# A three-stage kernel's weight preparation merged into its attention block, with the weights' peaks taken in the stage before and one restacking transfer moved ahead of another

## The chip, the cores and the metric

The kernel runs on one core of one Trainium2 chip. The metric is the device time of one execution in microseconds (us); lower is better. A core has a matrix engine (TensorE, here PE, with its weight loads as PEld), a vector engine (VectorE, DVE), a scalar engine (ScalarE, ACT), GpSimd (POOL), and SyncE (SP), which here only issues DMAs. Each runs its own instruction list in order, and they wait for each other through semaphores.

## The reference

```
h = ssm_kernel(log_dt, Lambda, x, L=1024)        # (32, 128, 1024), real part of a sum over 64 modes
h = concatenate([h, txt], axis=1)                # (32, 205, 1024)
h = h + attention(layernorm(h), wq, wk, wv, wo)  # 32 query heads, 8 key heads, head size 32, causal
h = h + ffn(layernorm(h), W_base, ...)           # a 1024x1024 map plus a low-rank one turned by an inverse FFT
```

wq is 1024x1024, wk and wv are 1024x256. `ssm_kernel` makes, for each of 32 images and 128 rows, 1,024 samples of a sum of decaying waves. The text has 77 rows an image, so an image has 205 rows in all.

## The kernel before

The program is a row of blocks. Within a block the engines run side by side; at its end all of them wait for each other.

**State-space block** (`ssm`). After some tables (the first 64 us) a loop over 16 chunks of 8 rows runs. In each chunk ACT copies a factor `ab` (L229), DVE multiplies two tables into `es` (L360) and adds the two halves of `u` (L364) that POOL made (L191, L192), PE multiplies them (L380), ACT copies the result out of PSUM to `ob` (L237) and SP stores it to `hcat` with four DMAs (L171). `es`, `u`, `ab` and `ob` have two buffers each, so ACT may write `ob` for chunk 2 only when the stores of chunk 0 have landed. Ahead of its stores SP issues the load of wq into `stage` (L166). Behind the loop DVE takes the largest absolute value of each partition of wq (L367).

**Weight block** (`prep_qkv`). SP loads wk and wv into `st_k` (L415, L416). A scale, a power of two, is made of each set's largest value over all partitions: POOL's PARTITION_ALL_REDUCE (L423), then five tiny DVE instructions. ACT writes the high fp16 part of the scaled weights in eight pieces a set (L430), and DVE the low part, what fp16 leaves over (L448).

**Attention block** (`attention`). A software pipeline over steps b from -4 to 32. In step b the engines load and normalise image b+4 or b+5, transpose image b+3 by DMA, project image b+2 to q, k and v (units "q", "k", "v" of 24 matmuls each), find the row maxima of the scores of image b+1 (units "m"), and do scores, exponentials and weighted sums for image b. A step has eight slots g; slots 0 to 3 carry an additional v or k unit. The normalisation goes round four engines: DVE statistics (L820 to L1072), POOL square-root rounds (L1079 to L687), ACT high part (L735, L737), DVE low part (L830), SP transposes (L648, L649), whose result PE takes in its first projection of step -2 (L982). `xfh` is a single buffer, and ACT casts a unit out of PSUM (L779) only behind what stands ahead of it in its list, in steps -3 and -2 the high part of the next image. PE has two PSUM banks for units, so the third unit waits until DVE has read the first (L861).

The projected rows lie four heads to a column of partitions, and SP restacks them (L596) for the score matmuls, since those want high, high and low parts of one head in one stack: 12 DMAs for each half of q (`qst`), 12 for each half of k (`kst`), 2 for the maxima of each half (L642, L643). All stand in SP's one list, 52 of them and four transposes a step. PE's row-maximum matmuls of the next step (L964) wait for the first halves of q and k, its score matmuls (L920) for the first maxima:

```
if has["qkv"]:
    wait(sp, pj_lo, base + at(rows, "q", 3) + 1)
    wait(sp, st_filled, 24 * b + 12)
    restack(Q_PARTS, qst[par], HALVES[0], q_in[0])
if has["max"]:
    wait(sp, pj_lo, base + at(rows, "m", 0) + 1)
    shift_rows(0, nxt)
if has["qkv"]:
    wait(sp, pj_lo, base + at(rows, "k", 0) + 1)
    restack(K_PARTS, kst[par], slice(0, 1), k_in[0])
```

`pj_lo` counts the units that DVE has split, `st_filled` the scores that PE has made. In step -1 SP also issues 15 loads for the blocks behind (L620). POOL fills constants at the start of the block (L658 to L681), and PE and ACT wait for them.

**Last blocks**: weight preparation for the output, then the output loop over 52 tiles of 128 rows.

## Time and profile before

| | us |
|---|---|
| median of 3 runs | 3023.08 |
| lowest and highest | 3008.07, 3027.96 |
| the profiled execution | 3040.87 |
| its span | 3039.1 |

The profile has the span, each engine's busy time, the time that each waited and for what, and the instructions in order of time. PE is the busiest engine. PEclk is the clock that was granted to PE, as a share of 2.4 GHz. By stage the span falls into the state-space block (0 to 184), the weight block (184 to 215), the attention block (215 to about 1,850) and the output blocks. The profiled execution took 17.8 us more than the median.

### The profile page before, as it was taken

The page shows a single profiled execution, that of the slowest core. Times are in us where ns is not written, and L with a number is a line of the kernel's source. Part 1 is how long each engine was busy: PE and PEld are TensorE (multiplying, and loading weights), DVE is VectorE, ACT ScalarE, POOL GpSimd, SP SyncE. Part 2 cuts the span into 40 slices and gives each one's busy share as a digit, 9 for nine tenths or more (in the row PEclk, how much of TensorE's full clock was granted, in tenths as well). Part 3 has the DMA queues.
Part 4 walks back from the last instruction along what each step waited for, and adds up shares of the span by engine and source line. Part 5 has one row for each costly group of instructions (what it writes and reads, how often), then busy time and mean ns, then how long its engine had stood idle before and what let it go on. Part 6 is the DMA issues. An engine that isn't in the chain of part 4 may idle for free. (4 is left out here: it accounts for less than half of the span.)

```text
span 3039.1 us, 71131 instructions
## 1 busy us (share of the span) xinstructions
PE 2733.4 (90%) x27520; PEld 1970.8 (65%) x27520; DVE 1939.9 (64%) x5548; ACT 1209.0 (40%) x2522; POOL 1145.9 (38%) x1816
## 2 busy tenths in 40 slices
PE   1934699999999999999999987699999999999999
PEld 1824689898898888888889873244444444444444
DVE  8863488888888878787787664444444444444443
ACT  4322265666766666666575664210110110110110
POOL 2731165665656656566565563011011011011010
PEclk9966799999999999999999976699999999999999
DMA  7642534343443443434334323254545545544543
GB/s 239 161 117 58 127 92 97 75 105 82 89 99 80 99 95 75 99 79 98 79 91 84 64 53 128 56 138 132 132 117 133 133 117 132 132 118 132 132 116 87
DMA packets 564063, 324.61 MB, mean 107 GB/s; under 512 B 500872, under 2 KB 519432, under 8 KB 563248
## 3 DMA queue, kind: packets, MB, share of 16 engines
q1 hardware_dynamic: 541216, 256.22, 36.4%
q10 hardware_dynamic: 22512, 63.84, 6.8%
q8 instruction: 220, 3.60, 0.5%
q14 instruction: 115, 0.94, 0.1%
HBM read 116.36 MB, written 80.61 MB: 65 GB/s over the span
## 5 line engine op out<-in xcount | busy, mean ns | idle before, releaser
L982 PE MATMUL psJ<-xth,qh 128*128 128x205 f16 x2048 | 524.3, 256 | 83.6 <-DMA xtl<-xfl 82.7
L707 POOL TENSOR_TENSOR pl<-p,ph 128x410 f16<-128x410 f32 (+1 forms) x512 | 506.9, 1010 | 95.6 <-ACT ph L771 95.6
L984 PE MATMUL psJ<-xth,ql 128*128 128x205 f16 x2048 | 522.8, 255 | 0.0
L983 PE MATMUL psJ<-xtl,qh 128*128 128x205 f16 x2048 | 522.7, 255 | 0.0
L702 POOL TENSOR_SCALAR_AFFINE_SELECT p<-p 128x256 f32<-128x256 f32 (+1 forms) x768 | 330.6, 436 | 496.2 <-ACT p L764 474.7
L1322 POOL TENSOR_TENSOR hb<-h,bias_sb 128x1024 f32<-128x1024 f32 x52 | 122.1, 2348 | 965.7 <-DVE h L1358 965.7
L764 ACT ACTIVATE p<-psT,escale 128x410 f32<-128x410 f32 (+1 forms) x768 | 400.9, 566 | 183.2 <-PE psT L923 118.7
L1336 ACT CAST xh<-xn 128x1024 f16<-128x1024 f32 x52 | 54.3, 1044 | 967.9 <-DVE xn L1367 967.9
L1397 PE MATMUL ps5O<-woh,ath 128*128 128x512 f16 x832 | 316.6, 381 | 28.2 <-DMA atl<-al 28.2
L771 ACT CAST ph<-p 128x410 f16<-128x410 f32 (+1 forms) x768 | 334.6, 500 | 13.0 <-POOL p L702 12.9
L1358 DVE SCALAR_TENSOR_TENSOR h<-ps5O,osc,h_in 128x512 f32<-128x512 f32 x104 | 78.0, 750 | 403.2 <-PE ps5O L1399 403.2
L853 DVE TENSOR_REDUCE mx<-psS 77x2 f32<-77x410 f32 x512 | 295.6, 577 | 54.3 <-PE psS L971 48.4
L847 DVE CUSTOM_DVE_ANT_0 seen<-psS,mask 128x128 bf16<-128x128 f32 x1024 | 235.7, 286 | 132.1 <-PE psS L964 132.0
L1398 PE MATMUL ps5O<-wol,ath 128*128 128x512 f16 x832 | 316.6, 381 | 0.0
L1397 PE MATMUL ps5F<-wfh,xth 128*128 128x512 f16 x832 | 315.4, 379 | 1.2 <-DMA xtl<-xl 1.2
L1399 PE MATMUL ps5O<-woh,atl 128*128 128x512 f16 x832 | 316.4, 380 | 0.0
L1399 PE MATMUL ps5F<-wfh,xtl 128*128 128x512 f16 x832 | 315.4, 379 | 0.0
L1398 PE MATMUL ps5F<-wfl,xth 128*128 128x512 f16 x832 | 315.4, 379 | 0.0
L950 PE MATMUL psO<-vh,ph 128*128 128x33 f16 (+1 forms) x3072 | 262.5, 179 | 4.6 <-issue 4.0
L982 PEld LDWEIGHTS psJ<-xth,qh 128*128 128x128 f16 x2048 | 202.1, 99 | 96.0 <-issue 83.0
L950 PE MATMUL psO<-vl,ph 128*128 128x33 f16 (+1 forms) x3072 | 261.3, 178 | 0.0
L950 PE MATMUL psO<-vh,pl 128*128 128x33 f16 (+1 forms) x3072 | 261.3, 178 | 0.0
(237 smaller groups left out, 6238.1 us busy)
## 6 DMA issues: line engine op xcount, KB each, us to landing
a_in<-acat SPq DMA_DIRECT2D x52, 512.0 KB, 3.8
h_in<-hcat SPq DMA_DIRECT2D x52, 512.0 KB, 4.7
qst<-qsh SPq DMA_DIRECT2D x512, 51.2 KB, 2.1
out<-y SPq DMA_DIRECT2D x51, 512.0 KB, 3.1
hcat<-ob SPq DMA_DIRECT2D x64, 256.0 KB, 4.0
xin<-hcat ACTq DMA_DIRECT2D x32, 512.0 KB
acat<-ao ACTq DMA_DIRECT2D x64, 256.0 KB
qst<-qsl SPq DMA_DIRECT2D x256, 51.2 KB, 2.1
```

Source lines behind the costliest of these rows:

```text
L702: pool.affine_select(out=v, in_=v, compare_op=ALU.is_ge, fill=0.0, base=0, pattern=[[0, v.shape[1]], [1, w]], channel_multiplier=-1).then_ ...
L707: pool.tensor_tensor(view(pl, g % 2, k), view(p32, g % 2, k), view(ph, g % 2, k), ALU.subtract).then_inc(lo_pool, 1)
L764: act.activation(view(p32, g % 2, k), ps_view(psT[(g + k) % 2], k), ACT.Exp, scale=(escale[:, 0:1] if k < 2 else escale[0:TXT, 0:1])).then ...
L771: act.copy(view(ph, g % 2, k), view(p32, g % 2, k)).then_inc(hi_done, 1)
L853: dve.tensor_reduce(dst, v, AX.X, ALU.max).then_inc(s_read, 1)
L950: m = pe.matmul(o[:, t, r, :], p, v[0:T[j], j, g, :], start=n == 0, stop=n == len(list_) - 1)
L982: pe.matmul(ps[:, 0:S], wh[:, k, c], xth[:, par, k, 0:S], start=k == 0, stop=False)
L983: pe.matmul(ps[:, 0:S], wh[:, k, c], xtl[:, par, k, 0:S], start=False, stop=False)
L984: m = pe.matmul(ps[:, 0:S], wl[:, k, c], xth[:, par, k, 0:S], start=False, stop=k == KC - 1)
L1397: pe.matmul(ps[h][:], th[:, k, :], wh[:, k, c], start=k == 0, stop=False)
L1398: pe.matmul(ps[h][:], th[:, k, :], wl[:, k, c], start=False, stop=False)
L1399: m = pe.matmul(ps[h][:], tl[:, k, :], wh[:, k, c], start=False, stop=k == KC - 1)
```

## The change

- SP issues the loads of wk and wv with that of wq, ahead of the stores of the state-space loop. `st_k` lies in a new buffer, `arena`, that attention's `p32` and `ao` and the output weights' `fm` use later. Five temporaries of the state-space block move into the unused half of `stage`.
- DVE takes the weights' peaks in twelve pieces of 128x1024, one at the end of each of the last twelve chunks. SP writes the two peaks of each partition to memory and reads all of them back into every partition ahead of the last chunk's stores.
- The weight block is gone. In the attention block DVE makes both scales at once from the peaks read back. ACT writes wq's high part behind the first two loads of rows, and that of wk and wv at the start of step -3; DVE writes the low parts behind the statistics of the first image and in slot 0 of step -3. PE waits for them ahead of its first two units.
- POOL no longer clears `xin`. The clearing of `ph` and `pl` moves to step -4 and that of a part of `p32` to step -3; `mask` is half as wide.
- In every step SP restacks the first half of the keys ahead of the first half of the queries, where before it came last. The wait for `st_filled` moves with it.

```
-def ssm(nc, x, txt, log_dt, lam, hcat, ahead, peak):
+def ssm(nc, x, txt, log_dt, lam, hcat, acat, ahead, st_k, peaks, all_peaks, peaks_in):
...
             sp.wait_ge(tab_ok, 4)
-            sp.dma_start(ahead[0], ahead[1]).then_inc(ahead[2], 16)
+            for dst, src, arrived in ahead:
+                sp.dma_start(dst, src).then_inc(arrived, 16)
             for ch in range(NCH):
+                if ch == NCH - 1:
+
+                    sp.wait_ge(peaks_ok, 1)
+                    sp.dma_start(acat[0, 0:2 * P].rearrange("(p t) -> p t", t=2), peaks[:]).then_inc(peaks_out, 16)
+                    sp.wait_ge(peaks_out, 16)
+                    sp.dma_start(all_peaks, acat[0:1, 0:2 * P].broadcast_to([P, 2 * P])).then_inc(peaks_in, 16)
 
                 sp.wait_ge(k_read, (ch + 1) * HC // 2)
...
+            def weight_peak(n):
+
+                if n == 0:
+                    dve.wait_ge(ahead[0][2], 16)
+                if n == 8:
+                    dve.wait_ge(ahead[1][2], 32)
+                src = ahead[0][0][:, n, :] if n < 8 else st_k[:, 2 * (n - 8):2 * (n - 8) + 2, :].rearrange("p k n -> p (k n)")
+                dve.tensor_reduce(pieces[:, n:n + 1], src, AX.X, ALU.max,
+                                  apply_absolute_value=True).then_inc(piece_ok, 1)
+
...
-            dve.wait_ge(ahead[2], 16)
-            dve.tensor_reduce(peak[:], ahead[0].rearrange("p k n -> p (k n)"), AX.X, ALU.max,
-                              apply_absolute_value=True)
+                if ch >= NCH - 12:
+                    weight_peak(ch - (NCH - 12))
+            dve.wait_ge(piece_ok, 12)
+            dve.tensor_reduce(peaks[:, 0:1], pieces[:, 0:8], AX.X, ALU.max)
+            dve.tensor_reduce(peaks[:, 1:2], pieces[:, 8:12], AX.X, ALU.max).then_inc(peaks_ok, 1)
...
+def attention(nc, ahead, hcat, acat, st, qkv, arena, all_peaks, peaks_in, ksc):
...
+                    sp.wait_ge(w_lo, 2 * KC)
...
                 if has["qkv"]:
 
+                    wait(sp, pj_lo, base + at(rows, "k", 0) + 1)
+                    wait(sp, st_filled, 24 * b + 12)
+                    restack(K_PARTS, kst[par], slice(0, 1), k_in[0])
                     wait(sp, pj_lo, base + at(rows, "q", 3) + 1)
-                    wait(sp, st_filled, 24 * b + 12)
                     restack(Q_PARTS, qst[par], HALVES[0], q_in[0])
                 if has["max"]:
 
                     wait(sp, pj_lo, base + at(rows, "m", 0) + 1)
                     shift_rows(0, nxt)
-                if has["qkv"]:
-
-                    wait(sp, pj_lo, base + at(rows, "k", 0) + 1)
-                    restack(K_PARTS, kst[par], slice(0, 1), k_in[0])
...
             pool.memset(mv[:], 1.0)
             pool.memset(xfh[:, 1, :], 0.0)
-            pool.memset(xfl[:, 1, :], 0.0)
-            pool.memset(xin[:, :, 1, :], 0.0).then_inc(cleared, 1)
+            pool.memset(xfl[:, 1, :], 0.0).then_inc(cleared, 1)
...
-            chain(pool.memset(ph[:], 0.0))
-            chain(pool.memset(pl[:], 0.0))
-            pool.memset(p32[:, :, 2, :], 0.0).then_inc(const_ok, 1)
+                m = pool.memset(vh[i][:, :, :, HD:HD + 1], 1.0)
+                if i < 2:
+                    chain(m)
+            m.then_inc(const_ok, 1)
...
+                    if b == -4:
+                        pool.memset(ph[:], 0.0)
+                        pool.memset(pl[:], 0.0)
+                    if b == -3:
+                        pool.wait_ge(w_lo, 2 * KC)
+                        pool.memset(p32[:, :, 2, :], 0.0).then_inc(late_ok, 1)
                     return
+                if b == 0:
+                    pool.wait_ge(late_ok, 1)
...
 
-            act.wait_ge(cleared, 1)
+            def weights_high(n):
+                if n == 0:
+                    act.wait_ge(scale_ok, 1)
+                for k in range(KC):
+                    act.activation(hi[n][:, k], st[n][:, k], ACT.Copy, scale=scs[n][:, 0:1]).then_inc(w_hi, 1)
+
             load(0, 0)
             load(1, 1)
-            act.wait_ge(const_ok, 1)
+            weights_high(0)
+            act.wait_ge(cleared, 1)
 
             def step(b, par, has):
                 base, k0 = before(b, par), odd(b, par)
                 rows = units(has)
                 n = 0
+                if b == -3:
+                    weights_high(1)
+                if b == -2:
+                    act.wait_ge(const_ok, 1)
+                if b == 0:
+                    act.wait_ge(late_ok, 1)
...
+            link = Chain(dve, w_c)
+            dve.wait_ge(peaks_in, 16)
+            link(dve.tensor_reduce(apeak[:], all_peaks.rearrange("p (q t) -> p t q", t=2), AX.X, ALU.max))
+            for n in range(2):
+                weight_scales(dve, link, apeak[:, n:n + 1], scs[n], tops[n])
+            link(dve.scalar_tensor_tensor(escale[:], scs[0][:, 1:2], float(HD) ** -0.5, ksc[:, 1:2], ALU.mult, ALU.mult))
+            dve.sem_inc(scale_ok, 1)
             dve.wait_ge(cleared, 1)
+
+            def weights_low(n):
+                for k in range(KC):
+                    dve.wait_ge(w_hi, n * KC + k + 1)
+                    dve.scalar_tensor_tensor(lo[n][:, k], st[n][:, k], scs[n][:, 0:1], hi[n][:, k],
+                                             ALU.mult, ALU.subtract).then_inc(w_lo, 1)
...
+                        if b == -4 and g == 3:
+                            weights_low(0)
                         for piece in {6: (0,), 7: (1, 2)}.get(g, ()):
                             low_part(b + 4, piece)
+                        if b == -3 and g == 0:
+                            weights_low(1)
...
+                                if b == -2 and n + which < 2:
+                                    pe.wait_ge(w_lo, KC * (n + which + 1))
```

The function `prep_qkv` is removed whole.

SP's list, in one step of the attention block before. `kst<-ksh` with `kst<-ksl` is a half of the keys, `qst<-qsh` with `qst<-qsl` a half of the queries, `mh` and `ml` are the maxima.

```order
L596 DMA qst<-qsh 32x4x205 [waits st_filled,pj_lo]
L596 DMA qst<-qsh 32x4x205 x7
L596 DMA qst<-qsl 32x4x205 x4
L642 DMA qst<-mh 1x16x205 [waits pj_lo]
L643 DMA qst<-ml 1x16x205
L596 DMA kst<-ksh 32x205 [waits pj_lo]
L596 DMA kst<-ksh 32x205 x3
L596 DMA kst<-ksl 32x205 x4
L596 DMA kst<-ksh 32x205 x4
```

And now:

```order
L571 DMA kst<-ksh 32x205 [waits st_filled,pj_lo]
L571 DMA kst<-ksh 32x205 x3
L571 DMA kst<-ksl 32x205 x4
L571 DMA kst<-ksh 32x205 x4
L571 DMA qst<-qsh 32x4x205 [waits pj_lo]
L571 DMA qst<-qsh 32x4x205 x7
L571 DMA qst<-qsl 32x4x205 x4
L616 DMA qst<-mh 1x16x205 [waits pj_lo]
L617 DMA qst<-ml 1x16x205
```

The 26 DMAs are the same; the keys now stand first and the maxima last.

```order
L678 MEMSET vh 128x16 [waits pool_c3] x3
L679 MEMSET ph 128x2460 [waits pool_c3]
L680 MEMSET pl 128x2460 [waits pool_c3]
L681 MEMSET p 128x2x410 [waits pool_c3]
L1079 ISA
L1079 TENSOR_TENSOR rs<-rs 128x2 [waits dve_ln]
```

And now the start of POOL's attention block, where the library change stands, and the end of its constants:

```order
L632 MEMSET mv 128x4
L633 MEMSET xfh 128x1024
L634 MEMSET xfl 128x1024
L635 MEMSET ident 128x128
L636 ISA [waits pool_c3]
L636 AFFINE_SELECT ident<-ident 128x128
```

```order
L648 MEMSET vl 128x528 [waits pool_c3]
L651 MEMSET vh 128x16 [waits pool_c3] x3
L1091 TENSOR_TENSOR rs<-rs 128x2 [waits dve_ln]
L1092 TENSOR_TENSOR rs<-rs 128x2 [waits pool_ln]
L1093 TENSOR_SCALAR rs<-rs 128x2 [waits pool_ln]
```

The change of library has moved from between the constants and the square root to near their start. The one for PARTITION_ALL_REDUCE in the weight block is gone with it.

DVE's list behind the scales now:

```order
L786 SCALAR_TENSOR_TENSOR escale<-qsc,ksc 128x1 [waits w_c]
L826 BN_STATS stats<-xin 128x6 [waits w_c,x_in0,cleared]
L826 BN_STATS stats<-xin 128x6 [waits dve_ln]
L827 BN_AGGR mv<-stats 128x2 [waits dve_ln]
L826 BN_STATS stats<-xin 77x6 [waits dve_ln] x2
L827 BN_AGGR mv<-stats 77x2 [waits dve_ln]
L1082 TENSOR_SCALAR rs<-mv 128x2 [waits dve_ln]
L1083 TENSOR_SCALAR rs<-rs 128x2 [waits dve_ln]
L1084 TENSOR_SCALAR rs<-rs 128x2 [waits dve_ln]
L793 SCALAR_TENSOR_TENSOR ql<-stage,qsc,qh 128x1024 [waits w_hi,dve_ln]
L793 SCALAR_TENSOR_TENSOR ql<-stage,qsc,qh 128x1024 [waits w_hi] x7
```

The low parts of the weights (`ql`) now stand behind the first image's statistics; before they stood ahead of the block.

## Rows read from the trace of the kernel before

**Rows 1.** Busy time by stage: start and end, length, then each engine, PEclk, DMA share.

```profile
177.00:260.00 83.00, 0.33 (x3) 0.24 (x3) 33.49 (x51) 20.86 (x28) 23.06 (x51) 0.53 0.30 79
...
400.00:1750.00 1350.00, 1286.88 (x19436) 1194.86 (x19437) 1081.10 (x3705) 876.70 (x1985) 814.27 (x1490) 0.99 0.40 87
```

**Rows 2.** Timeline of the weight block: start, duration, engine, line, instruction, count, [idle before, releaser].

```profile
184.56 0.40 SPq L415 DMA_DIRECT2D st_k<-in_L_attn_wk  x1
...
192.73 0.38 POOL L423 PARTITION_ALL_REDUCE apeak<-peak_q  x1 [24.34 <-issue]
...
209.94 5.38 DVE L448 SCALAR_TENSOR_TENSOR kl<-st_k,ksc,kh 128x512 f16<-128x512 f32 x8
```

**Rows 3.** Timeline of POOL from the attention block's start to the first square root's start.

```profile
215.58 0.10 POOL L658 MEMSET mv<- 128x4 f32 x1 [16.51 <-POOLq L403]
...
217.40 1.81 POOL L661 MEMSET xin<- 128x2048 f32 x1
...
219.50 0.29 POOL L663 TENSOR_SCALAR_AFFINE_SELECT ident<-ident 128x128 f32<-128x128 f32 x1 [0.16 <-POOL ident L662]
...
228.30 0.62 POOL L678 MEMSET vh<- 128x16 f16 x3
...
240.93 0.18 POOL L1079 TENSOR_TENSOR rs<-rs 128x2 f32<-128x2 f32 x1 [6.76 <-issue]
```

**Rows 4.** Timeline of all engines: the first two images up to PE's third unit.

```profile
249.44 0.72 ACT L737 ACTIVATE xfh<-xin,rs 77x512 f16<-77x512 f32 x1
...
254.65 0.17 DVE L1072 TENSOR_SCALAR rs<-rs 128x2 int32<-128x2 int32 x1
...
258.21 0.21 POOL L687 TENSOR_SCALAR nmean<-mv 128x2 f32<-128x2 f32 x1
...
259.77 0.33 PE L982 MATMUL psJ<-xth,qh 128*128 128x205 f16 x1 [82.67 <-DMA xtl<-xfl]
...
263.31 0.72 ACT L737 ACTIVATE xfh<-xin,rs 77x512 f16<-77x512 f32 x1
...
266.26 0.25 PE L982 MATMUL psJ<-xth,qh 128*128 128x205 f16 x1
```

**Rows 5.** PE's waits from 400 to 1,750 us: total, times, longest.

```profile
PE psS L964 <- issue: 31.8, 26, 2.5
```

**Rows 6.** Timeline of one step, its third slot to the next step's start.

```profile
1085.42 1.28 SPq L649 DMA_TRANSPOSE xtl<-xfl  x1
...
1088.21 0.36 DVE L861 TENSOR_TENSOR ksl<-psJ,ksh 128x205 f16<-128x205 f32 x1
...
1092.14 0.36 DVE L861 TENSOR_TENSOR qsl<-psJ,qsh 128x205 f16<-128x205 f32 x1
1092.52 1.95 SPq L596 DMA_DIRECT2D qst<-qsh  x3
...
1113.40 0.58 PE L964 MATMUL psS<-kst,qst 96*128 96x128 f16 x4 [1.75 <-issue]
```

**Rows 7.** Timeline: two rows of the state-space loop, a peak, an instruction beside a memset.

```profile
82.17 0.59 ACT L237 COPY ob<-ps 128x512 f32<-128x512 f32 x1 [0.86 <-PE ps L380]
...
88.25 2.29 DVE L360 TENSOR_TENSOR es<-tab,ab 128x2048 f32<-128x2048 f32 x1 [1.29 <-ACT ab L229]
...
194.20 4.42 DVE L438 TENSOR_REDUCE peak_k<-st_k 128x1 f32<-128x4096 f32 x1
...
227.71 0.56 DVE L1071 TENSOR_SCALAR rs<-rs 128x2 int32<-128x2 int32 x1
```

**Rows 8.** DMA issues, 75 to 80 us and 184 to 195 us: count, size each, us to landing.

```profile
hcat<-ob SPq DMA_DIRECT2D x2, 256.0 KB, 5.2
...
st_k<-in_L_attn_wv SPq DMA_DIRECT2D x1, 1024.0 KB, 8.5
```

**Rows 9.** Durations of two lines: ns min/median/max, first and last start.

```profile
L351 DVE TENSOR_TENSOR tab<-tab,stage x4: 2291/4613/4618, 42.3 to 53.6; 128x2048 f32<-128x2048 f32 x4
...
L192 POOL TENSOR_TENSOR u<-wi,gg x16: 2527/2529/4574, 46.9 to 165.9; 128x1024 f32<-128x1024 f32 x16
```

More of the change, by code:

```diff
@@ L134, in ssm @@
         stored = [sem("stored0"), sem("stored1")]
+        pieces = sb("pieces", [P, 12])
+        piece_ok, peaks_ok, peaks_out = sem("piece_ok"), sem("peaks_ok"), sem("peaks_out")
         def by_mode(w, ch):
@@ L452, in attention @@
-def attention(nc, ahead, hcat, acat, qh, ql, kh, kl, escale):
+def attention(nc, ahead, hcat, acat, st, qkv, arena, all_peaks, peaks_in, ksc):
     T = (P, TXT)
@@ L1430, in build @@
             kh, kl = sb3("kh", [P, KC, 2 * KW]), sb3("kl", [P, KC, 2 * KW])
-            qsc, escale = sb3("qsc", [P, 4], F32), sb3("escale", [P, 1], F32)
-            prep_qkv(nc, stage, peak, wk, wv, qh, ql, kh, kl, qsc, ksc, escale)
             ahead = [(stage[:], by_chunk(wo), staged), (enc[0:R0, :], enc0, in_small), (enc[R0:R, :], enc1, in_small)]
@@ L1437, in build @@
                     ahead.append((mk[n][:, :, e, :], by_chunk(m[e]), in_small))
-            attention(nc, ahead, hcat, acat, qh, ql, kh, kl, escale)
+            attention(nc, ahead, hcat, acat, (stage, st_k), (qh, ql, kh, kl), arena, all_peaks, peaks_in, ksc)
         osc, fsc = sb("osc", [P, 4], F32), sb("fsc", [P, 4], F32)
```

97 lines of the change are left out of this document (31 added, 66 removed).

## The prediction

> **What bounds the kernel now.** I read the busy time by stage first. In the long part of the attention block, 400 to 1,750 us, PE is busy 1,287 of 1,350 us, so it has 63 us to give. Between the state-space loop and the first projection, 177 to 260 us, it does nothing [rows 1]. So a change can win at most the 83 us of that gap and 63 us in the loop, and this change touches both.
>
> Next the timeline of the gap, which is one chain. The weight block starts at 184.6, its first scale waits for POOL until 192.7, and DVE ends at 215.3 (209.94 + 5.38) [rows 2]. Then the attention block starts. POOL fills constants until 228.9, clears three buffers until about 234.2 and stands for 6.76 us ahead of its first small multiply, for which the profile names no releaser. A square root takes 3.6 us (for the second image 254.82 to 258.42), so the first is ready at 244.5 [rows 3, 4]. From there it is 15.3 us over ACT, DVE and the transposes to PE's first matmul at 259.77 [rows 3, 4]. None of DVE's statistics is on that path.
>
> Last, PE's waits in the loop. One of them has half of PE's idle time: the first row-maximum matmuls of a step, 31.8 us in 26 waits, the longest 2.5 [rows 5]. The profile gives no releaser, but the code has one: they wait for the first half of the keys, which SP issues last. In the step shown SP starts the chain (queries, maxima, keys) at 1092.52, right behind the split of unit q3 (1092.14 + 0.36), and PE starts at 1113.40 after 1.75 us of idle time [rows 6].
>
> **The change, part by part.** Times are in the profiled execution's own scale.
>
> *State-space loop.* A peak over 4,096 elements took 4.42 us [rows 7], so one over 1,024 takes 1.1 to 1.25 us. DVE is idle 1.29 us in each chunk [rows 7] at just the place where the peak now stands. It fits, and I cost it at 0; if it takes 1.4 us instead, twelve chunks lose about 1 us. The 8.7 us reduction over all of wq that goes ran beside the last chunks and the last stores and was worth nothing.
> The two loads are not free. They took 8.5 us to land on an idle queue, of which about 6 are transfer [rows 8], and the stores of chunk 0 now queue behind them. Those landed 5.2 us after the issue [rows 8], at about 81 us (the last issue was near 76), and ACT took the buffer again at 82.17 without waiting for them [rows 7]. Landing at 87, ACT comes back 5 us late. PE has four PSUM banks of cover, some 5 us, and loses a few tenths; ACT's factor for chunk 4 comes 1.6 us late, against about 0.4 us of slack on DVE. I take 1.3 us lost, once (bounds 0 and 3). The peaks' way through memory is some 0.5 us in front of the last stores. The attention block so starts at 184.6 + 1.8 = 186.4.
>
> *POOL's start.* POOL is the late one there, since the scales need no DMA and no all-reduce in this block and are ready some 2.5 us in. Up to `ident` it took 3.9 us with the memset of `xin` (1.81), which goes: 2.1, so 188.5. There the library change now stands. It is what I read the 6.76 us as; the other change in the trace, ahead of the all-reduce, took at most 8.2 (184.6 to 192.73, beside the loads of wk and wv) [rows 2, 3]. I take 7.2, as row loads run beside it: 195.7. The constants took 9.4 us (219.50 to 228.92) [rows 3], less 0.6 for the halved mask: 204.5.
> But now DVE writes wq's low parts beside them, eight instructions of 1.2 us, from about 196 to 206. Before, no low part ran beside a constant. The nearest rows speak for a price: the table multiply with two operands in SBUF takes 2.29 us alone and 4.61 beside POOL's multiply, and that goes from 2.53 to 4.57 [rows 9]; and a DVE instruction on two columns took 0.56 us beside POOL's memsets, where its like took 0.17 [rows 4, 7]. So they seem to take turns. Each of the eight low parts then holds POOL up by about 1 us. Bounds 0 and 9.7; I take 8, by these rows. The constants end at 212.5, and the square root, 3.6 us as before, at 216.1.
> The Trainium skill, in "GPSIMD Engine Reference", section "Specifications", says that GpSimd shares its SBUF interfaces with VectorE and that they contend when a DVE instruction has two SBUF inputs. The low part has two. The rows above agree for POOL's multiplies; whether a memset, which reads nothing, is held up as well, no row shows with such an instruction. By the page the whole 9.7 would be lost, without it nothing.
>
> *First images.* In the trace before, image 1's square root came 1.4 us ahead of PE's start (258.42 and 259.77). Now, counted from image 0's square root: ACT's high parts end at +5.7 (250.16 - 244.49), DVE's low parts at +7.3 behind POOL's moved memsets, wk's and wv's low parts take 5.4 more (as DVE's last row of the weight block), statistics 3.9, square root 3.6: +20.2. ACT's four high parts take 5.6 us (up to 264.03), then come unit q0's cast, DVE's last low part and split: +27. Only then may PE start its third unit. Its first could start at +16, its second ends at +22.5, so PE waits some 4.5 us in between. The third unit started at 266.26 [rows 2 to 4], now at 216.1 + 27 = 243.1: 23.1 us gained. Restarting from such a pause, PE gets the lower of its two clocks, 1.2 GHz: in the gap the granted clock was 0.53 [rows 1]; a start cost about 1.5 us. Left: 21.6.
>
> *Keys first, in the filling.* The keys can go about 2 us earlier in step -2, since k0 is split one unit ahead of q3. In step 0 the maxima now come last and PE's first scores wait for them: about 1 us lost, and another 1 by the exponential table's load. Sum 0.
>
> *Keys first, in the loop.* k0 is split at 1088.57 and q3 at 1092.50 [rows 6], and SP has been waiting since its last transpose, 1086.7 (1085.42 + 1.28) [rows 6]. So the chain of 26 DMAs starts 3.9 us earlier, and q3 is ready long before its turn. It ends with the maxima, whose landing may take 0.6 us longer than that of keys: last landing 3.3 us earlier. Even the longest wait, 2.5 us, with the 0.35 us that the scores stand ahead of it, is covered. PE's 31.8 us [rows 5] should go. Some of it comes back, since ACT and DVE used the pause to catch up; some clock dips go with it, the mean granted clock being 0.99 [rows 1]. I take 29 us, bounds 8 (others take over) and 39 (all of it and the dips).
>
> **The sum.** 21.6 + 0 + 29 = 50.6 us. 3040.87 - 50.6 = 2990.3 for the profiled execution; that one stood 17.8 above the median, so 3023.08 - 50.6 = 2972.5 for the median. About 1%, 30 us, is what a measurement of this kernel can tell from no change.
>
> **Rivals.**
> 1. *Others take over in the loop.* PE's other 31 us of idle time show that ACT and DVE are near behind. If they fill most of the pause, the loop gives 8 and not 29: 2993.5. Against it: slots 0 to 3, where the pause is, are PE's longest, and ACT and DVE have room there.
> 2. *No taking turns.* Memsets don't hold DVE up and POOL's constants take what they took: 8 us more gained, 2964.5. For it: the fill of `vh` beside DVE's statistics kept its length. Against it: rows 7 and 9.
> 3. *The merged start is slower than reckoned*: a longer library change, 3 us lost in the loop of chunks, a second cold start. Some 14 us less, 2986.5.
> 4. *Slower: the maxima become the gate.* `mh` and `ml` are now SP's last issues, and they gate not only the row maxima but the step's first scores, and with them exponentials and everything behind. If SP's chain does not start earlier, because SP is still busy with transposes when k0 is split, each step gets 0.35 + 0.6 us for the later last landing and about 1 us for exponentials that no longer run in the pause: 31 steps by 1.95 = 60 us lost. 3023.1 - 21.6 + 60 = 3061.5. It decides where the chain starts less than about 1 us earlier. Against it: SP stood idle 5.8 us ahead of the chain in the step shown (1086.7 to 1092.52) [rows 6].
>
> **Chances.** The forecast 0.55, rival 1 0.17, rival 2 0.15, rival 3 0.09, rival 4 0.04. The time is that of the forecast, 2972.5. Its bounds: all terms at their best end give 8 + 1.3 + 10 = 19 us more, 2953, and some 8 for the scatter of the runs, 2946; at their worst 1.7 + 1.7 + 1 + 21 = 25 less, 2998, and a part of the scatter, 3003. That range takes in rivals 1 to 3. Faster by over 1% (below 2992.9): nearly all of the forecast, rivals 2 and 3 and half of rival 1, 0.84; within 1% 0.12; slower 0.04.
>
> **What would show each step.** In the trace of the changed kernel: ACT's first copy of chunk 2 some 5 us late and PE with a gap of about a microsecond near 95 us; no gap in the last twelve chunks; POOL's idle time of about 7 us behind `ident`; POOL's constants at 1.5 to 2 times their length beside `ql`; PE's first unit near 232 and its third near 243 with 4 to 5 us of idle time ahead of it; SP starting the keys right behind the split of k0; no wait left at the row maxima's first matmul, and none above a few tenths at the scores' (L920 before). I would be wrong if steps kept their 47 us, or if a wait for `ml` stood at each step's start.

## The result, and the profile after

The median of four runs is 2978.19 us (2973.98 to 2981.47), against 3015.57 for four runs of the kernel before beside them (3002.17 to 3027.96). The ratio is 0.9861, with a 95% interval of 0.9826 to 0.9896: faster by over 1%. The predicted 2972.5 is 5.7 us off. A second series, with 14 runs of the kernel before, gave 2968.8 for the changed kernel and 0.9813 (0.978 to 0.9847). Each kernel shows two times about 20 us apart (last section): all four runs of the changed kernel in the first series stand at its longer one, half of the four before; at equal level the gain is 47 us in the first series and 50 to 54 in the second.

The total was nearly right, but two of its terms were off by about 10 us each, in opposite directions. That shows only stage by stage.

The busy time by stage of the kernel after, with the columns of [rows 1]:

```profile
177.00:260.00 83.00, 31.26 (x294) 29.24 (x292) 40.67 (x78) 33.16 (x53) 29.69 (x61) 0.69 0.38 83
400.00:1700.00 1300.00, 1245.44 (x19005) 1161.79 (x19002) 1054.29 (x3622) 859.02 (x1938) 791.33 (x1463) 1.00 0.42 89
```

PE now works 31 us of the gap. In the loop it is idle 55 us of 1,300, or 4.2%; before it was 63 of 1,350, or 4.7%. That is a smaller step than a wait of 31.8 us that goes should make. The gap first, on POOL (to set beside [rows 3]):

```profile
187.78 0.10 POOL L632 MEMSET mv<- 128x4 f32 x1 [18.27 <-POOLq L77]
...
190.03 0.29 POOL L636 TENSOR_SCALAR_AFFINE_SELECT ident<-ident 128x128 f32<-128x128 f32 x1 [0.24 <-POOL ident L635]
...
198.38 0.61 POOL L651 MEMSET vh<- 128x16 f16 x3
198.90 1.04 POOL L1091 TENSOR_TENSOR rs<-rs 128x2 f32<-128x2 f32 x1
200.02 1.12 POOL L1092 TENSOR_TENSOR rs<-rs 128x2 f32<-128x2 f32 x1
...
208.40 0.19 POOL L1091 TENSOR_TENSOR rs<-rs 128x2 f32<-128x2 f32 x1
...
209.51 0.25 POOL L660 TENSOR_SCALAR nmean<-mv 128x2 f32<-128x2 f32 x1
...
211.78 2.14 POOL L670 MEMSET pl<- 128x2460 f16 x1
```

Look for two things. There is no idle time of 7 us anywhere, behind `ident` or elsewhere. And the same small multiply takes 1.04 to 1.12 us at 199 to 208 and 0.19 at 208.40. DVE and PE in the same stretch (to set beside [rows 4]):

```profile
198.61 9.66 DVE L793 SCALAR_TENSOR_TENSOR ql<-stage,qsc,qh 128x1024 f16<-128x1024 f32 x8
211.35 0.75 DVE L836 SCALAR_TENSOR_TENSOR xfl<-xin,rs,xfh 128x512 f16<-128x512 f32 x1 [3.09 <-ACT xfh L718]
212.72 0.75 DVE L836 SCALAR_TENSOR_TENSOR xfl<-xin,rs,xfh 128x512 f16<-128x512 f32 x1 [0.61 <-ACT xfh L718]
```

```profile
226.16 0.33 PE L992 MATMUL psJ<-xth,qh 128*128 128x205 f16 x1 [47.94 <-DMA xtl<-xfl]
...
235.71 0.26 PE L992 MATMUL psJ<-xth,qh 128*128 128x205 f16 x1 [3.04 <-DVE qsl L867]
```

The slow multiplies stand beside `ql`, whose instructions read two buffers; the memset of `pl` (211.78, 2.14 us) stands beside `xfl` (212.72), and neither is longer than its like elsewhere. PE's third unit starts at 235.71, 30.6 us earlier than before.

PE's waits in the loop, 400 to 1,700 us (total, times, longest), for [rows 5], and in the filling, 240 to 400 us:

```profile
PE psS L978 <- DVE mx L853: 38.0, 54, 1.1
PE psT L933 <- ACT arena L757: 13.9, 38, 1.8
```

```profile
PE psS L978 <- DVE mx L859: 13.9, 1, 13.9
PE psT L930 <- DMA qst<-ml: 11.6, 1, 11.6
PE psS L974 <- DMA qst<-qsl: 5.7, 1, 5.7
```

The keys' wait is gone whole. But the wait for DVE's row maxima, which in the kernel before was this one row over 400 to 1,750 us, has grown from 15.0 to 38.0:

```profile
PE psS L968 <- DVE mx L847: 15.0, 40, 1.1
```

SP's list in one step (for [rows 6]) shows why the keys' wait went: the keys start at 1099.79 and the first queries 8.4 us behind them, and the maxima come last.

```profile
1099.79 2.48 SPq L571 DMA_DIRECT2D kst<-ksh  x4
...
1108.15 5.92 SPq L571 DMA_DIRECT2D qst<-qsh  x8
1114.11 2.75 SPq L571 DMA_DIRECT2D qst<-qsl  x4
1116.91 0.60 SPq L616 DMA_DIRECT2D qst<-mh  x1
```

Two marks split the whole into start, loop and rest: PE's first and last weighted-sum matmul. Of the kernel before and of the kernel after, from their timelines of PE:

```profile
371.91 0.18 PE L950 MATMUL psO<-vh,ph 128*128 128x33 f16 x1
...
1850.04 0.19 PE L950 MATMUL psO<-vh,pl 77*128 77x33 f16 x1
```

```profile
339.26 0.18 PE L960 MATMUL psO<-vh,ph 128*128 128x33 f16 x1
...
1792.58 0.19 PE L960 MATMUL psO<-vh,pl 77*128 77x33 f16 x1
```

The start gave 32.6 us and not 21.6. The loop is 1,453 us long, and 1,478 in the profiled run of the kernel before. How much of these 25 the change made is not to be had from two profiles; e1 to e4 say it.

The busy time inside the loop shows what the rows of waits do not. Here are its first 28 images and its last four, before and after (columns as in [rows 1]):

```profile
371.91:1702.10 1330.19, 1267.80 (x19154) 1176.98 (x19153) 1073.67 (x3669) 867.63 (x1961) 806.33 (x1484) 0.99 0.41 89
1702.10:1850.04 147.94, 128.67 (x1979) 109.51 (x1978) 87.20 (x341) 91.75 (x210) 94.28 (x152) 0.77 0.23 55
```

```profile
339.26:1651.30 1312.04, 1255.81 (x19155) 1170.98 (x19154) 1073.14 (x3669) 870.46 (x1961) 800.76 (x1484) 1.00 0.42 90
1651.30:1792.58 141.28, 122.60 (x1979) 105.21 (x1978) 86.73 (x341) 91.73 (x210) 92.69 (x152) 0.83 0.24 57
```

PE does the same work, but is busy 18 us less for it (1,396.5 and 1,378.4 us), at a higher granted clock, while its idle time falls by 7 us only (81.7 and 74.9). The kernel before falls to half the clock for a few microseconds in some steps. The step of [rows 6] is one of them, where PE starts at 1113.40 behind an idle time of 1.75 us:

```profile
1113.00:1117.00 4.00, 3.60 (x25) 3.30 (x26) 1.85 (x11) 0.30 (x2) 0.92 (x3) 0.57 0.09 22
```

### The profile page after: what moved, and what is told of

It is laid out like the page before. It is cut to its first block and busy times, and to the rows that moved or that the text cites. A ratio compares the mean times of both kernels' runs of the same rounds, so it can differ in the third digit from the quotient of the medians.

```text
span 2979.7 us, 71132 instructions
## 1 busy us (share of the span) xinstructions
PE 2714.5 (91%) x27520; PEld 1960.1 (66%) x27520; DVE 1940.0 (65%) x5561; ACT 1211.3 (41%) x2522; POOL 1142.8 (38%) x1813
## 5 line engine op out<-in xcount | busy, mean ns | idle before, releaser
L992 PE MATMUL psJ<-xth,qh 128*128 128x205 f16 x2048 | 520.1, 254 | 51.9 <-DMA xtl<-xfl 47.9
L688 POOL TENSOR_TENSOR pl<-arena,ph 128x410 f16<-128x410 f32 (+1 forms) x512 | 499.9, 996 | 95.5 <-ACT ph L764 95.5
L683 POOL TENSOR_SCALAR_AFFINE_SELECT arena<-arena 128x256 f32<-128x256 f32 (+1 forms) x768 | 330.4, 436 | 476.8 <-ACT arena L757 455.2
L757 ACT ACTIVATE arena<-psT,escale 128x410 f32<-128x410 f32 (+1 forms) x768 | 401.7, 567 | 123.1 <-PE psT L933 60.8
L764 ACT CAST ph<-arena 128x410 f16<-128x410 f32 (+1 forms) x768 | 334.5, 500 | 13.5 <-POOL arena L683 13.4
L960 PEld LDWEIGHTS psO<-vh,ph 128*128 128x128 f16 (+1 forms) x3072 | 245.8, 97 | 6.7 <-issue 6.6
```

The costliest lines, as they stand in the source:

```text
L683: pool.affine_select(out=v, in_=v, compare_op=ALU.is_ge, fill=0.0, base=0, pattern=[[0, v.shape[1]], [1, w]], channel_multiplier=-1).then_ ...
L688: pool.tensor_tensor(view(pl, g % 2, k), view(p32, g % 2, k), view(ph, g % 2, k), ALU.subtract).then_inc(lo_pool, 1)
L757: act.activation(view(p32, g % 2, k), ps_view(psT[(g + k) % 2], k), ACT.Exp, scale=(escale[:, 0:1] if k < 2 else escale[0:TXT, 0:1])).then ...
L764: act.copy(view(ph, g % 2, k), view(p32, g % 2, k)).then_inc(hi_done, 1)
L960: m = pe.matmul(o[:, t, r, :], p, v[0:T[j], j, g, :], start=n == 0, stop=n == len(list_) - 1)
L992: pe.matmul(ps[:, 0:S], wh[:, k, c], xth[:, par, k, 0:S], start=k == 0, stop=False)
```

## The experiments

Twelve kernels ran. Line numbers shift by two to four between them.

### One part of the change at a time (e1 to e4)

e1 is the kernel before with the changed order of SP's list, e2 the changed kernel with the old order. e3 and e4 are the kernel after and before once more, to see how far two profiles of one kernel lie apart. The edit of e1, in `step` on SP:

```
                 if has["qkv"]:
 
+                    wait(sp, pj_lo, base + at(rows, "k", 0) + 1)
+                    wait(sp, st_filled, 24 * b + 12)
+                    restack(K_PARTS, kst[par], slice(0, 1), k_in[0])
                     wait(sp, pj_lo, base + at(rows, "q", 3) + 1)
-                    wait(sp, st_filled, 24 * b + 12)
                     restack(Q_PARTS, qst[par], HALVES[0], q_in[0])
...
-                if has["qkv"]:
-
-                    wait(sp, pj_lo, base + at(rows, "k", 0) + 1)
-                    restack(K_PARTS, kst[par], slice(0, 1), k_in[0])
```

> The kernel before with SP's order alone changed (keys, queries, maxima). Theory (the loop's wait for the keys goes, little takes its place): about 20 us less than the kernel before in the median, since the profile showed 25 us between the first and the last weighted sum and the kernel before was profiled in one of its longer executions; the wait at the row maxima's first matmul gone, the state-space and weight blocks unchanged, the first 370 us within 2 us. Rival (the maxima become the gate): 0 to 60 us more, with a wait for ml at each step's start. Second rival (other waits take the place, only ACT's and DVE's): within 8 us of before, with DVE's maxima as PE's wait grown by the 30 us that the keys' wait lost.

> The changed kernel with SP's order put back (queries, maxima, keys). Theory: the merge alone is worth what PE's third unit came earlier, 30 us (266.26 to 235.71), so 28 to 32 us less than before, and the wait at the row maxima's first matmul is back, 10 to 32 us in the loop. Rival (part of the merge's gain is lost again in the filling because SP's loads for the later blocks stand there anyway): 20 us or less. The two parts, this run and the one with the keys alone, should add up to the whole within 5 us if they are independent.

> The changed kernel again, on the same chip as the two halves. Theory: 40 to 50 us less than the kernel before, its executions within 5 us of each other, since the wait whose length varied is gone; 2974 to 2982 us.

> The kernel before, profiled once more. Its executions lie between 3002 and 3041 us. Theory (the spread is the length of the wait for the keys): an execution near 3010 us has 30 us less than the one profiled, and its wait at the row maxima's first matmul is below 15 us in total instead of 31.8. Rival (the spread comes from somewhere else, such as the clock or the output loop): the wait is near 30 us whatever the time.

Measured, in us, the kernel before at 3030.68 beside them:

| | median | ratio, 95% interval | first weighted sum | loop | PE busy, idle in it |
|---|---|---|---|---|---|
| before (profile of the first series) | | | 371.9 | 1478.1 | 1396.5, 81.7 |
| e4, before again | 3023.8 (one run) | | 369.1 | 1465.9 | 1388.7, 77.2 |
| e1, keys first alone | 3007.75 | 0.994, 0.992 to 0.9959 | 369.6 | 1455.1 | 1376.7, 78.5 |
| e2, merge alone | 2998.33 | 0.9901, 0.9866 to 0.9935 | 338.4 | 1472.0 | 1393.1, 78.9 |
| after (profile of the first series) | | | 339.3 | 1453.3 | 1378.4, 74.9 |
| e3, after again | 2968.8 | 0.9813, 0.978 to 0.9847 | 338.9 | 1451.1 | 1378.3, 72.7 |

By these marks the parts add. The three profiles without the merge start their weighted sums at 370.2 on average, the three with it at 338.8: 31.4 us. The three loops without keys first are 1472.0 long, the three with it 1453.2: 18.8 us. Neither touches the other's number. (The medians alone, 22.9 and 32.4 against 61.9, miss the 5 us that I had allowed, since half of e3's runs stand at the shorter of its two times; against those at the longer one the whole is 53.5.) The waits of e2 in the loop are those of the kernel before:

```profile
PE psS L976 <- issue: 32.6, 26, 2.2
PE psS L980 <- DVE mx L855: 13.4, 37, 1.1
```

So the wait for the maxima grows only when the keys' wait goes (39.3 us in e1). The last column says what the 18.8 us are: on average PE's idle time falls by 3.9 us and its busy time, for the same work, by 14.9. Cut into windows of 50 us from 400 to 1,700 us, the granted clock is below 1.00 in seven windows of the kernel before, in three of e4 and in four of e2, and in none of e1, after or e3. The order of SP's list alone makes this difference, with the merge and without it. So the pauses for the keys cost PE clock as well as time, and most of what their removal gave came from there. The last four images, where the clock is low for longer in all six, give some 6 of the 14.9 us; why they do was not tried.
Two profiles of one kernel differ by 12 us in the loop (before and e4), though their waits for keys differ by under 3 (30.4 and 27.7 us between 400 and 1,700); 7.8 of the 12 are busy time, again with more windows at a low clock. No single pair of profiles can size a term of 20 us. The theory of e4, that the spread is the length of the wait for the keys, is so not borne out (17 us shorter as a whole, 2.7 us less of that wait), and e3's forecast of runs within 5 us of each other failed: they span 22.

### The library of POOL (e5)

```
+            chain(pool.memset(spare_in[:], 1.0))
+            chain(pool.partition_all_reduce(spare_out[:], spare_in[:], P, RMAX))
             pool.memset(mv[:], 1.0)
```

> The changed kernel with one all-reduce over a throwaway 128x1 tile at the head of POOL's attention block, everything else as it is. Theory A (POOL pays for its library only on the way into and out of the all-reduce's, and both payments went when the all-reduce went): about 8 us more before the first identity mask, made of the switch in and the reduce of about 0.1 to 0.2 us, and 6 to 7 us of idle in front of the first tensor_tensor of the square root; the square root of image 0 is ready 13 to 15 us later than 209.8, so near 224, and PE's first product and third unit about 10 to 15 us later. Rival B (a library change is free in this kernel wherever it stands now, and the 8.1 and 6.8 us of before were something else, such as waiting for the peaks): the reduce takes under 1 us, no idle over 1 us ahead of the square root, milestones within 2 us of the changed kernel's.

POOL's timeline:

```profile
185.17 0.10 POOL L633 MEMSET spare_in<- 128x1 f32 x1 [17.48 <-POOLq L77]
192.58 0.38 POOL L634 PARTITION_ALL_REDUCE spare_out<-spare_in  x1 [7.31 <-issue]
...
195.20 0.29 POOL L639 TENSOR_SCALAR_AFFINE_SELECT ident<-ident 128x128 f32<-128x128 f32 x1 [0.16 <-POOL ident L638]
...
211.71 0.18 POOL L1094 TENSOR_TENSOR rs<-rs 128x2 f32<-128x2 f32 x1 [7.53 <-issue]
```

Theory A holds: one all-reduce on one column costs 7.31 us ahead of it and 7.53 us ahead of the first multiply behind it, though memsets, the mask and a cast stand between. The first multiply pays for the way back, not `ident`. Its sizes for what follows were too large: the square root is ready at 215.0 and not near 224, since the block started 2.6 us earlier and the multiplies, now behind `ql`, were short again (209.8 + 15.2 - 2.6 - 7.3 = 215.1), and PE's third unit starts at 241.28, some 6 us later than in the kernel after and e3 (235.7, 235.2), or 8 counted from the block's start, and not 10 to 15. The page "GPSIMD Engine Reference" of the Trainium skill, section 2.1, "Instruction dispatch", says that the first call to a freshly loaded kernel pays about 6 us without a visible instruction. The rows agree in kind, with 7.3 and 7.5 us, and show the way back as a second payment.

### The square root beside DVE (e6)

```
+                            dve.wait_ge(ln_done, 1)
                             weights_low(0)
```

> The changed kernel, with the low parts of wq on DVE waiting until POOL has left the statistics of image 0. Theory A (the two-input operations of DVE hold back each of POOL's small tensor_tensor operations to one per DVE operation, 0.93 us): the square root of image 0 takes 3.6 us as in the kernel before instead of 10.9, ready about 7 us earlier, near 202.5; the low parts then start at about 202.5 instead of 198.6, still ahead of the first centred image, and PE's third unit moves by less than 4 us either way. Rival B (the stretching comes from something else on POOL, such as the gathered statistics arriving or the transfers of the low parts): the square root still takes 9 us or more.

```profile
197.42 0.19 POOL L1092 TENSOR_TENSOR rs<-rs 128x2 f32<-128x2 f32 x1
...
200.76 0.25 POOL L660 TENSOR_SCALAR nmean<-mv 128x2 f32<-128x2 f32 x1
```

With `ql` held back the square root takes 3.6 us again, so `ql` was what stretched it to 10.9. PE's third unit gains 2 us against the block's start at most (232.96 - 186.28 = 46.7, against 47.2, 47.9 and 48.6 in e2, after and e3): DVE's low parts of wq, now from 201 to 211, stand ahead of the first image's as before. The 7.3 us on POOL so cost PE little.
The page "SBUF — State Buffer" of the Trainium skill, section "Who interferes with whom", states the rule exactly: a DVE instruction with two SBUF inputs contends with a GpSimd instruction that reads SBUF, and not with one that only writes. The trace agrees on both halves, with multiplies at 1.12 us instead of 0.19 and a memset of 2.14 us that stays so. e6 shows the second half more cleanly, since there POOL's two memsets stand beside `ql` (201.11 to 210.76) and take the 2.15 us each that they took in the kernel before:

```profile
200.95 2.15 POOL L669 MEMSET ph<- 128x2460 f16 x1
203.04 2.15 POOL L670 MEMSET pl<- 128x2460 f16 x1
```

### The loads and the peaks in the state-space loop (e7, e8)

e7 issues the loads of wk and wv in chunks 4 and 6. e8 has ACT issue the two DMAs of the peaks.

```
-            for dst, src, arrived in ahead:
-                sp.dma_start(dst, src).then_inc(arrived, 16)
+            sp.dma_start(ahead[0][0], ahead[0][1]).then_inc(ahead[0][2], 16)
             for ch in range(NCH):
+                if ch in (4, 6):
+                    dst, src, arrived = ahead[ch // 2 - 1]
+                    sp.dma_start(dst, src).then_inc(arrived, 16)
```

> The changed kernel, with the loads of wk and wv issued in chunks 4 and 6 of the state-space loop instead of all three weights up front. Theory A (the 5.9 us that ACT waited for the gathers of chunk 2, and with it PE's gaps near 87.8 and 95, is the price of 1.5 MB of weights landing at once): ACT's wait in chunk 2 falls under 2 us, PE's gap of 0.6 us there goes, and the state-space loop on PE is 0.5 to 1.7 us shorter than 114.9. Rival B (the wait is there for the chunk's own gathers): the wait of ACT remains 4 us or more and the loop is as long as before within 0.3 us.

> The changed kernel, with the write and the spreading read of the peaks issued from ACT's queue inside the last chunk's results instead of from SP's queue, where they stand behind the transfers of chunk 14. Theory A (the round trip is late because it stands in SP's queue behind those transfers, issued at 175.0 though the peaks were ready at 172.9): written about 2 us earlier, and the attention block on POOL starts 1 to 3 us earlier than 187.8. Rival B (ACT reaches its issue no earlier, or the block's start is bound by the last chunk's gathers and not by the peaks): start within 0.5 us of 187.8.

In the kernel after ACT waits for the stores of chunk 0, and PE then shortly for ACT:

```profile
87.03 2.05 ACT L246 COPY ob<-ps 128x512 f32<-128x512 f32 x4 [5.88 <-DMA hcat<-ob]
...
87.76 7.14 PE L401 MATMUL ps<-es,u 128*128 128x256 f32 x32 [0.61 <-ACT ob L246]
```

In e7 that wait does not occur, and PE runs through:

```profile
79.71 30.59 PE L403 MATMUL ps<-es,u 128*128 128x256 f32 x141
```

DVE's last instruction on the peaks starts at 169.9 in e7, at 170.2 to 172.2 in the kernels with the loads up front: 0.3 to 2.3 us for the loads. The prediction's 1.3 lies inside, but one profile of e7 can't size it. In e5 and e6 ACT's wait was 4.1 and 3.6 us and PE had no gap either, in e3 5.3 without one, so PE's four banks cover up to some 5 us. e8 is inconclusive: POOL's block starts at 185.24, inside the 185.07 to 187.78 of the kernels without the edit, and 15.0 us behind the peaks as there (14.6 to 15.6). The write did leave earlier, 0.9 us behind the peaks and not 2.8, but the read back was issued at 177.45, as in e2 and e5 (177.66, 177.41), and held up ACT's copy by 2.71 us. My reading that the peaks' place in SP's queue sets the start is not borne out.
The single runs took 2984.0 us (e5), 2978.9 (e6), 2972.3 (e7) and 2955.1 (e8); e8's is short mainly because its block of output weights ran at the higher clock (last section), not by its edit.

### What took the keys' place (e9)

From image 4 on DVE takes the rows' low part (`xfl`, four instructions in slots 6, 7 and 0 of each step) over 32 columns instead of 512; the rest is left out.

```
+                if m >= 4:
+                    c = slice(c.start, c.start + 32)
                 dve.scalar_tensor_tensor(xfl[0:r, t, c], xin[0:r, m % 2, t, c], rs[0:r, 3, t:t + 1], xfh[0:r, t, c],
```

> The changed kernel with the low part of the rows (xfl, four operations of up to 1.1 us on DVE in each step) taken over 32 columns instead of 512 from image 4 on; the rest of the low part is left out. Theory A (with the keys early, what PE waits for in the loop is DVE, late at the row maxima because of these low parts, and this took the place of the keys' wait): PE's waits for the row maxima between 400 and 1700 fall from 38 us to under 12, and the loop from the first to the last weighted sum, 1453 us in the changed kernel, is 20 to 30 us shorter. Rival B (the maxima are late by their own chain from the scores, or ACT's exponentials take over): the waits stay above 25 us or others take their place, and the loop is under 8 us shorter.

```profile
PE psS L980 <- DVE mx L855: 21.7, 26, 0.8
PE psT L935 <- ACT arena L757: 13.5, 39, 1.6
```

The one run took 2957.3 us. Its loop is 1433.6 us (335.56 to 1769.12), 19.8 shorter, and the wait for the maxima fell from 38 to 21.7 us. The mechanism is A's, at a bit less than its size: some 16 of the 38 us are the low parts. PE's idle time in the loop falls by 15.2 us and its busy time by 4.6. POOL's busy time falls too, from 893 to 854 us, so what comes by way of DVE alone is not separated. What makes the other 22 was not tried. That in the kernel before DVE caught up with the low parts in the pause for the keys is my reading of these numbers; no run tests it by itself.

### The loads in the filling (e10)

```
-                if b == -1:
-
-                    sp.wait_ge(w_lo, 2 * KC)
-                    for dst, src, arrived in ahead:
-                        sp.dma_start(dst, src).then_inc(arrived, 16)
...
                     shift_rows(0, nxt)
+                if b >= 0:
+                    if b == 0:
+                        sp.wait_ge(w_lo, 2 * KC)
+                    for dst, src, arrived in ahead[2 * b:2 * b + 2]:
+                        sp.dma_start(dst, src).then_inc(arrived, 16)
```

> The changed kernel with the fifteen loads for the next block, all issued from SP's queue in step -1 (24.5 us of it, 279.7 to 304.2), issued two at the end of each step from step 0 on. Theory A (these loads cause the two long waits of the filling, 11.6 us for the low sums and 13.9 us for the row maxima): both waits fall under 4 us, and the first weighted sum starts 12 to 22 us earlier than 339; the loop of 1453 us is not longer by more than 3. Rival B (the filling is bound by the projections and their gathers whatever SP sends between): the first weighted sum moves by less than 5 us, or the loads spread cost the loop as much as they gave in the filling.

PE's waits from 240 to 400 us, and its first weighted sum:

```profile
PE psT L930 <- DMA qst<-ml: 6.0, 1, 6.0
PE psS L974 <- DMA qst<-qsl: 5.5, 1, 5.5
```

```profile
312.48 0.18 PE L960 MATMUL psO<-vh,ph 128*128 128x33 f16 x1
```

The one run took 2957.0 us. The wait of 13.9 us for the maxima is gone, that for `ml` went from 11.6 to 6.0 (under 4 was expected), and the weighted sums start 26.8 us earlier than in the kernel after, at a loop that stays 1454.7 long. 2.4 of them are an earlier start of the block (185.42), so the edit gave some 24, and so did the whole: 2957.0 against 2981.47 us for the profiled run of the kernel after, with the same clock in the block of output weights. That is more than the whole merge was predicted to give, and it stood in the trace of before as 25 us of SP's list between restacks (311.25 to 336.40).

### The three edits together (e12)

e12 has the edits of e7, e8 and e10.

> The changed kernel with the three edits that helped in runs before: the next block's loads spread over the steps (first weighted sum 26 us earlier there), wk and wv loaded in chunks 4 and 6, and the peaks carried by ACT's queue. Theory A (the gains add, since the first lies in the filling and the others before the attention block): attention block starts on POOL at 184.5 to 185.5, first weighted sum at 308 to 312, the time 2930 to 2955 us by the level of the clock in the Fourier block, median 2945, ratio to the kernel before 0.970 to 0.978. Rival B (the earlier start only lengthens the waits of the filling for gathers and maxima): first weighted sum no earlier than 312, median 2955 or more.

The median of six runs is 2952.44 us (2933.03 to 2955.02), the ratio to the kernel before 0.9752, with an interval of 0.9721 to 0.9784. The first weighted sum starts at 312.79, so of theory A the ratio came, and POOL's block started at 184.96 as expected, but the weighted sums came no earlier than in e10 (312.48). The third unit waits longer than in the kernel after or e10 (3.04, 1.45 us), yet starts 1.35 us earlier than in e10 (233.18); the rest of the head start is lost behind it, at a place that was not looked for.

```profile
231.83 0.35 PE L994 MATMUL psJ<-xth,qh 128*128 128x205 f16 x1 [4.33 <-DVE qsl L869]
```

Nearly all of it is e10's edit. It beats both kernels: five of its six runs took 2949.6 to 2955.0 us, where those of the changed kernel that compare with them (last section) took 2974 to 2981, so about 25 us.

### Feeding PE (e11)

See the last section for what this tests.

```
+            def keep_busy(n):
+                for _ in range(n):
+                    pe.matmul(psA[0][:], stage[:, 0, 0:P], stage[:, 0, 0:HALF], start=True, stop=True)
+
+            pe.wait_ge(staged, 32)
+            keep_busy(6)
             pe.wait_ge(in_small, SMALL_LOADS * 16)
             pe.wait_ge(cm_ok, 1)
             for k in range(KC):
+                keep_busy(1)
                 pe.wait_ge(in_f[k], 16)
```

> The changed kernel with products whose result is never read on PE in the Fourier block: six of 128x512 in f32 while it waits for the first rows, and one before each of the eight chunks of G. Theory A (the two times that each kernel shows, about 20 us apart, come from TensorE's clock in this block: 32 groups of products take 1.64 us each at the full clock, 3.05 us at the half, and which it is hangs on how busy PE was before): the block stays at the full clock in every run, the time is 2950 to 2965 us and its spread over the runs under 6 us. Rival B (the clock falls there for another reason, such as the power that these very products draw): both levels still appear, or only the low one, and the time is 2970 us or more.

Three of four runs took 2963.84, 2968.97 and 2988.21 us; the fourth took 12,261, which nothing here explains, and it is left aside. The ratio is 0.9835 (0.9785 to 0.9886), no better than without the edit. The three lie 24 us apart where under 6 was expected, so theory A's remedy falls. The one profile (2968.97) has the higher clock in the block, and from the last weighted sum to the first product of the output loop takes 90.8 us, against 83.2 and 80.9 in e3 and e8: the extra products cost 8 to 10 us.

## Why the prediction was right or wrong

- *State-space loop, 1.3 us lost; block 1.8 us later.* Right in mechanism and about in size: ACT 5.88 us late, PE's gap 0.6 and not 1, the peaks in DVE's idle time (1.21 us each) without a gap. The block starts at 185.0 to 187.8 in the eleven profiles with the merge, and the weight block at 182.7, 183.6 and 184.6 in e1, e4 and before: some 2 us later on average, with a scatter as large.
- *"There the library change now stands", 7.2 us: wrong.* I took the 6.76 us ahead of the first multiply for a price of getting POOL's ordinary library at all, to be paid once wherever the first such instruction stands. e5 shows that it is the way back out of the all-reduce's. With the all-reduce gone both payments go; the change of library near the start of the list, which I had taken for a move of the payment, costs nothing (0.24 us ahead of `ident`). This is the largest miss of the start.
- *"Each of the eight low parts then holds POOL up", 8 us on the constants: the price was right, the victim wrong.* The constants, 190.03 to 198.99, were not slowed, and but for the last 0.4 us they did not even stand beside `ql`, which began at 198.61; e6 shows that memsets beside it lose nothing, so on them rival 2 was right. The square root behind them was slowed, by 7.3 us. The 0.56 us of [rows 7] is another pair, a DVE instruction with one input beside a memset; it stands in the kernel after too, at 197.79, and says nothing of the low parts. The even sum is luck. The two bounds I gave, all or nothing on memsets, left out that the reads behind them pay.
- These steps account for the square root: 216.1 - 7.2 - 8 + 7.3 + 1.4 (block start) = 209.6, and it was ready at 209.76.
- *Third unit 27 us behind it: right*, 25.95, with 3.04 us of idle time ahead of it (4.5 predicted).
- *A cold clock costs 1.5 us: right, if it is meant for the restart at the third unit.* The first unit starts at a low clock in both kernels (0.63 from 259 to 265 us before, 0.71 from 226 to 232 after), so there it is no difference. But behind the 3.04 us of idle time ahead of the third unit the clock falls again; in the kernel before, which has no such pause, it is 1.00 from 265 to 275 us. A mean of 0.57 over the 4 us of this row is 3.4 us at half speed, which cost PE about 1.7 us:

```profile
236.00:240.00 4.00, 4.00 (x28) 3.61 (x27) 1.56 (x4) 0.33 (x1) 0.00 (x0) 0.57 0.66 118
```

- *Keys first, 0 in the filling*: right within 2 us. e2 and e3 start their weighted sums at 338.4 and 338.9, from blocks that start at 185.07 and 186.55.
- *Keys first, 29 us in the loop: mis-sized, and wrong in what pays.* It gave 18.8. SP issues the keys right behind the split of k0 (1099.79, split done at 1099.76), and the keys' wait went whole, as worked out. But "some of it comes back" was taken at 3 us, and nearly all of it did: the wait for the maxima grew by 23 us, in the profile before it was already the second longest, and PE's idle time fell by 3.9 us on average. Rival 1's mechanism (others take over) was at work at nearly full strength. The forecast was not missed by more because of the term that it named and gave no size, "some clock dips go with it": that is the 14.9 us of busy time. That the two make up two thirds of 29 is luck as well.
- Rival 4 (the maxima become the gate) is refuted: between 400 and 1,700 us the kernel after has no wait for `ml`.
- *The sum*: 31.4 + 18.8 = 50.2 us measured, 50.6 predicted, from 21.6 and 29. The total is right because +10 and -10 met. I would not claim it as understanding.

## What to carry to other kernels

A wait that is taken away was also a pause in which other engines caught up: price its removal by what stands second in the list of waits, and ask of each engine how much work it has deferred into the pause. Look at the busy time of the same work and at the granted clock, too: here 30 us of waiting that went gave 4 us of idle time and 15 of a faster PE. An idle time ahead of an instruction "for nothing" belongs to the instruction that changed the engine's state, and it goes with that one. And read a queue's list in the filling of a pipeline with the same care as in its loop: fifteen loads in one place cost some 24 us, more than the whole merge was forecast to give.

## What the runs showed that I had not expected

Both kernels show two times, some 20 us apart: the changed one 2958 to 2961 and 2974 to 2981, the one before 3002 to 3012 and 3020 to 3034 (its profiled execution, 3040.87, stands above both, with the longest loop of the table). In the changed kernel's profiles the place is the block that prepares the output weights, where PE does 32 groups of one f32 product and four transposes. The kernel after and e3, the same program, from 1,820 to 1,840 us (columns as in [rows 1]) and one product of each:

```profile
1820.00:1840.00 20.00, 19.27 (x43) 8.12 (x44) 7.79 (x9) 3.84 (x7) 0.00 (x0) 0.59 0.00 0
...
1827.38 2.07 PE L1169 MATMUL psA<-gt,enc 40*128 40x512 f32 x2
```

```profile
1820.00:1840.00 20.00, 20.00 (x73) 8.74 (x74) 13.69 (x17) 6.77 (x12) 0.00 (x0) 1.00 0.00 0
...
1828.09 1.12 PE L1169 MATMUL psA<-gt,enc 40*128 40x512 f32 x2
```

At a granted clock of 1.00 (2.4 GHz) a pair of these products takes 1.12 us, at 0.50 (1.2 GHz) 2.07, and the stretch from the block's first product to the first of the output loop 75.0 us in e3 (1798.14 to 1873.18) and 93.9 in the kernel after (1800.74 to 1894.68). Where it takes the longer time, the clock falls while PE is working without a pause, about 23 us into the block (1824.3), after an idle time of 8 us ahead of it and a low clock in the last step of attention. The kernel after and e8 had nearly the same pauses up to there (7.96, 0.78 and 2.27 us; 7.94, 0.81 and 1.87 us), and one fell and the other did not. Of all fourteen profiles e3, e8 and e11 are at the higher clock there. The kernel before was not profiled at its shorter time, so that its two times have the same cause is not shown. What decides it stays open; more products on PE ahead of the place (e11) did not bring the runs to one time. So a comparison of these kernels below 20 us needs runs of the same level on both sides, or the marks ahead of that block, as used above.
